# Four small moves in a decoder layer: a residual one tick sooner, the third norm in front of a gate product, epsilon on VectorE, the next input turned in front of the last attend

## The chip, the cores and the metric

The kernel runs on one core of a Trainium2 chip. The metric is the device time of one execution in microseconds; of several executions the median counts.

## The reference

A decoder layer in fp32 over 16 batches of 128 tokens and 256 channels, with three parts, each behind a LayerNorm and added to a residual:

```python
x = x + attn(layernorm(x))             # r, k, v, g from inputs mixed with the token before; 32 heads of 8
x = x + xattn(layernorm(x), ctx)       # causal softmax attention on ctx, 16 heads of 16
x = x + ffn(layernorm(x))              # 8 experts of 176, top 2 of them, and a shared one of 704
# layernorm: (x - mean) / sqrt(var + 1e-5)
# attn, inputs: xx = shift(x) - x;  xk = x + xx * maa_k (xv, xr, xg alike)
# attn, heads: att = (r k) * decay; y = att v; group norm per head; y * silu(g) @ Wo
# ffn: silu(x @ gate) * (x @ up), times the expert's weight, @ down
```

## The kernel before

The 16 batches are worked off in four waves (`g` = 0 to 3) of four batches, 512 tokens. A wave goes through the first attention, the cross attention and the router. The feed-forward part of wave `g - 1` is cut into 34 pieces of 128 hidden rows (`FN` = 34, 17 for each half of 256 tokens) and dealt out between the steps of wave `g`, as *ticks*. That of the last wave runs behind everything, on its own. Each engine has its program written out by hand, in order; `point(g, name)` is the place at which an engine does the ticks that `COUNT` gives to that name. The points are n0 to n5, then x0a, x0b, x0c and so on to x3c for the four batches of the cross attention, then y0 and r0 to r3. Wave 0 has no ticks; there the points do the splitting of the feed-forward weights into high and low parts.

A tick n is a chain over the engines. TensorE does the gate and up products of piece n (L1001 to L1003, 12 products), then the down products of piece n - 2 (L1039 to L1041). ScalarE takes the silu (L772), VectorE multiplies by the up part (L1442, called the gate product here), POOL multiplies by the expert's weight (L612), ScalarE makes the high part (L762), POOL the low part (L601), and that is what the down products wait for. The down products of a half of 17 pieces add up in one PSUM bank. VectorE adds them to the residual when the half is done (L1437), and the first down product of the next half waits for that, since it starts the same bank anew.

The cross attention does, for each batch, scores, maxima, exponentials (ScalarE, L879), the causal selection (POOL, L666) and the product `attend` (TensorE, L1249). On VectorE `attended` takes a reciprocal (L1558) and a multiplication (L1560) that write `yT`. The output projection (TensorE, L1177) waits for `yT` of all four batches. In between, the input of the next wave is made ready: normalised, transposed on TensorE (`turn_norm`, L962, 8 products into banks 2 and 3), then copied by ScalarE (L722) and VectorE (L1384), and `input_differences` subtracts the neighbouring tokens on VectorE (L1386, L1388). The copies wait for `edge_zero`, a memset of the edge column on POOL (L552), which POOL does behind its ticks of x3c.

A LayerNorm takes statistics on VectorE (`bn_stats`, `bn_aggr`), adds epsilon on POOL (L542), raises to the power -0.5 on POOL (L544) and applies mean and factor on VectorE (L1358). The third norm of a wave comes behind the output projection; its result is transposed too (L962), and makes the input of the feed-forward part: `xTf` high by ScalarE (L905), low by VectorE (L1612). Behind the transposes TensorE does the down products of pieces 31 and 32 and the first projection of the next wave (L997), and later the router's product (L1298).

Of the kernel before, what the change touches and what calls it, by code (L numbers as in the profile page):

```python
# [17 lines left out]
def decoder_layer(nc, x, ctx_in, Wr, br, Wk, bk, Wv, bv, Wg, bg, Wo, bo, ln_g, ln_b,  # L18
# [11 lines left out]
    GB = 4  # L30
# [7 lines left out]
    FN = 2 * FB  # L38
    TICKS = FN + 3
    LN_EPS = 1e-5  # L40
# [4 lines left out]
    with es:  # L45
# [341 lines left out]
        POINTS = ["n0", "n1", "n2", "n3", "n4", "n5"] + [f"x{b}{p}" for b in range(GB) for p in "abc"] + ["y0", "r0", "r1", "r2", "r3"]  # L387
        COUNT = dict(n0=1, n1=2, n2=2, n3=2, n4=2, n5=1, y0=1, r0=2, r1=1, r2=1, r3=2)
        for b in range(GB):
# [112 lines left out]
        def _(pool):  # L502
# [35 lines left out]
            def layer_rstd(s, g):  # L538

                i = 0 if s == 0 else 1  # L540
                pool.wait_ge(ln_mean[s], g * 4 + 4)
                pool.tensor_scalar(ve[:, i, :], mv[:, i, :, 1], LN_EPS, None, ALU.add).then_inc(ln_var[s], 1)  # L542
                pool.wait_ge(ln_var[s], g + 1)
                pool.tensor_tensor(rstd[:, i, :], ve[:, i, :], mhalf[:], ALU.pow).then_inc(ln_rstd[s], 1)  # L544
# [391 lines left out]
        def _(pe):  # L936
# [135 lines left out]
            for g in range(NG):  # L1072
# [180 lines left out]
                if g == 0:  # L1253
                    query_scores(0)
                    query_scores(1)
                    for b in (0, 2):
                        turn_maxima(b)
                        key_scores(b)
                        turn_maxima(b + 1)
                        key_scores(b + 1)  # L1260
                        attend(b)
                        attend(b + 1)
                        if b == 0:
                            query_scores(2)
                            query_scores(3)
                else:
                    for b in range(GB):
                        query_scores(b)
                        point(g, f"x{b}a")
                        turn_maxima(b)  # L1270
                        point(g, f"x{b}b")
                        key_scores(b)
                        point(g, f"x{b}c")
                        attend(b)

                if g + 1 < NG:
                    turn_norm(0, g + 1, tokx, 2)
                point(g, "y0")
# [50 lines left out]
        def _(dve):  # L1329
# [10 lines left out]
            def half_means(s, g, q):  # L1340
                i = 0 if s == 0 else 1
                dve.wait_ge(ln_stats[s], g * 4 + 2 * q + 2)
                for b in (2 * q, 2 * q + 1):
                    nc.vector.bn_aggr(mv[:, i, b, :], st[:, i, b, :]).then_inc(ln_mean[s], 1)

            def layer_stats(s, g, src):
# [4 lines left out]
                for b in range(GB):  # L1351
                    nc.vector.bn_aggr(mv[:, i, b, :], st[:, i, b, :]).then_inc(ln_mean[s], 1)

            def layer_apply(s, g, src, dst):
# [77 lines left out]
            def ffn_tick(f, n):  # L1432
                if n - 3 in (FB - 1, FN - 1):
                    half = (n - 3) // FB
                    dve.wait_ge(down_done, f * FN + (half + 1) * FB)
# [18 lines left out]
            for g in range(NG):  # L1454
# [108 lines left out]
                if g == 0:  # L1563
# [10 lines left out]
                    point(g, "x2a")  # L1574
                    attended(2)
                    attended(3)
                else:
                    for b in range(GB):
# [6 lines left out]
                        if b == 2 and g + 1 < NG:  # L1585
                            layer_apply(0, g + 1, tokx, tokx)
                        point(g, f"x{b}c")
                        attended(b)
                point(g, "y0")
                if g + 1 < NG:  # L1590
                    input_differences(g + 1)

# [8 lines left out]
                if g + 1 < NG:  # L1601
                    mixed_input(g + 1, 0)
                if g:
                    ffn_tick(g - 1, ticks_at(g, "r0")[1])
                layer_apply(2, g, X, tok2)
                point(g, "r1")
# [93 lines left out]
```

## Time and profile before

| | |
|---|---|
| median of three runs | 670.97 us (670.49 to 671.01) |
| profiled execution | 671.46 us; span from first to last instruction 669.7 us |
| mean granted TensorE clock | 0.985 |
| TensorE (PE) busy | 621.6 us, 93% |
| VectorE (DVE) busy | 382.8 us, 57% |
| GpSimd (POOL) busy | 342.1 us, 51% |
| ScalarE (ACT) busy | 269.3 us, 40% |

Only TensorE is busy nearly all the time. An engine that is busy for half of the span matters where TensorE waits for it. The granted clock is given as a share of full speed; 0.5 is the lower of its two levels, 1.2 GHz instead of 2.4.

### The profile page before, as it was taken

The page shows a single profiled execution, that of the slowest core. Times are in us where ns is not written, and L with a number is a line of the kernel's source. Part 1 is how long each engine was busy: PE and PEld are TensorE (multiplying, and loading weights), DVE is VectorE, ACT ScalarE, POOL GpSimd, SP SyncE. Part 2 cuts the span into 40 slices and gives each one's busy share as a digit, 9 for nine tenths or more (in the row PEclk, how much of TensorE's full clock was granted, in tenths as well). Part 3 has the DMA queues.
Part 4 walks back from the last instruction along what each step waited for, and adds up shares of the span by engine and source line. Part 5 has one row for each costly group of instructions (what it writes and reads, how often), then busy time and mean ns, then how long its engine had stood idle before and what let it go on. Part 6 is the DMA issues. An engine that isn't in the chain of part 4 may idle for free.

```text
span 669.7 us, 16176 instructions
## 1 busy us (share of the span) xinstructions
PE 621.6 (93%) x6680; PEld 496.7 (74%) x6680; DVE 382.8 (57%) x780; ACT 269.3 (40%) x608; POOL 342.1 (51%) x468
## 2 busy tenths in 40 slices
PE   7987977799999899999999899999999999999996
PEld 6544455445989799755888799854798889899996
DVE  5997778678734453769642544769752444552220
ACT  3857123132335455242325545342324545343332
POOL 7583164214445656514455565615364545518766
PEclk8999978899999999899999999999999999999999
DMA  7921000010121111002031111002011111015220
GB/s 193 357 56 33 1 1 2 1 63 7 39 71 37 42 55 42 5 17 65 27 86 26 38 56 41 21 16 66 18 54 35 37 44 52 21 36 123 70 69 16
DMA packets 41827, 34.13 MB, mean 51 GB/s; under 512 B 9901, under 2 KB 41206, under 8 KB 41754
## 3 DMA queue, kind: packets, MB, share of 16 engines
q1 hardware_dynamic: 39850, 31.27, 16.7%
q10 hardware_dynamic: 1904, 1.84, 0.8%
q8 instruction: 52, 0.85, 0.5%
q14 instruction: 21, 0.17, 0.1%
HBM read 30.92 MB, written 2.17 MB: 49 GB/s over the span
## 4 chain that ended last, share of the span: by engine, by line
PE 47%; DVE 20%; POOL 14%; ACT 8%; issue 8%; DMA 2%; ACTq 0%; POOLq 0%; DVEq 0%
PE bank L997 7%; DVE A L1467 6%; PE bank L1001 4%; DVE nm L1544 3%; POOL A L689 3%; PE bank L1002 3%; PE bank L1003 3%; POOL hT_last L698 3%; PE bank L1177 3%; POOL hb L612 3%; PE bank L1249 3%; PE bank L1039 3%; ACT A L879 2%; PE bank L994 2%; PE bank L1194 2%
## 5 line engine op out<-in xcount | busy, mean ns | idle before, releaser
L1442 DVE TENSOR_TENSOR hb<-hb,bank 128x256 f32<-128x256 f32 (+1 forms) x102 | 42.7, 419 | 144.5 <-ACT hb L772 144.1
L612 POOL TENSOR_TENSOR hb<-hb,cwb 128x256 f32<-128x256 f32 (+1 forms) x102 | 76.4, 749 | 79.1 <-DVE hb L1442 79.0
L601 POOL TENSOR_TENSOR hT<-hb,hT 128x256 fp32r<-128x256 f32 (+1 forms) x102 | 79.3, 778 | 73.2 <-ACT hT L762 73.2
L762 ACT ACTIVATE hT<-hb 128x256 fp32r<-128x256 f32 (+1 forms) x102 | 42.4, 416 | 122.9 <-POOL hb L612 122.3
L1001 PE MATMUL bank<-xTf,wGh 128*128 128x256 f32 x272 | 83.1, 305 | 0.0
L1467 DVE TENSOR_TENSOR A<-bank,decay 128x512 f32<-128x512 f32 x128 | 77.2, 680 | 7.0 <-PE bank L1095 7.0
L1002 PE MATMUL bank<-xTf,wGh 128*128 128x256 f32 x272 | 76.7, 282 | 0.0
L1003 PE MATMUL bank<-xTf,wGl 128*128 128x256 f32 x272 | 76.6, 282 | 0.0
L1002 PE MATMUL bank<-xTf,wUh 128*128 128x256 f32 x256 | 72.2, 282 | 0.0
L1003 PE MATMUL bank<-xTf,wUl 128*128 128x256 f32 x256 | 72.1, 282 | 0.0
L1001 PE MATMUL bank<-xTf,wUh 128*128 128x256 f32 x256 | 72.1, 282 | 0.0
L566 POOL TENSOR_TENSOR A<-A,mcol 128x512 f32<-128x512 f32 x32 | 34.9, 1098 | 72.5 <-PE bank L1095 63.1
L1039 PE MATMUL bank<-wDh,hT 128*128 128x256 f32 (+1 forms) x204 | 59.8, 293 | 5.5 <-DVE res L1437 4.7
L772 ACT ACTIVATE hb<-bank 128x256 f32<-128x256 f32 (+1 forms) x102 | 38.2, 374 | 60.5 <-PE bank L1003 60.1
L1040 PE MATMUL bank<-wDl,hT 128*128 128x256 f32 (+1 forms) x204 | 57.7, 283 | 0.0
L1041 PE MATMUL bank<-wDh,hT 128*128 128x256 f32 (+1 forms) x204 | 57.6, 282 | 0.0
L1001 PEld LDWEIGHTS bank<-xTf,wGh 128*128 128x128 f32 x272 | 51.4, 189 | 8.3 <-issue 5.6
L1002 PEld LDWEIGHTS bank<-xTf,wGh 128*128 128x128 f32 x272 | 51.4, 189 | 0.2
L1003 PEld LDWEIGHTS bank<-xTf,wGl 128*128 128x128 f32 x272 | 51.1, 188 | 0.0
L1001 PEld LDWEIGHTS bank<-xTf,wUh 128*128 128x128 f32 x256 | 48.3, 189 | 0.0
L1002 PEld LDWEIGHTS bank<-xTf,wUh 128*128 128x128 f32 x256 | 48.2, 188 | 0.0
L1003 PEld LDWEIGHTS bank<-xTf,wUl 128*128 128x128 f32 x256 | 48.1, 188 | 0.0
(210 smaller groups left out, 1407.9 us busy)
## 6 DMA issues: line engine op xcount, KB each, us to landing
cwb<-cw_rows SPq DMA_DIRECT2D x54, 128.0 KB, 2.9
A<-cw_rows SPq DMA_DIRECT2D x18, 128.0 KB, 3.4
A<-in_x SPq DMA_DIRECT2D x4, 512.0 KB, 4.5
res<-in_x SPq DMA_DIRECT2D x4, 512.0 KB, 4.1
out_x<-res SPq DMA_DIRECT2D x8, 256.0 KB, 2.5
rawG<-in_L_ffn_w_gate SPq DMA_DIRECT2D x2, 704.0 KB, 6.2
rawU<-in_L_ffn_w_up SPq DMA_DIRECT2D x2, 704.0 KB, 6.6
cwb<-cw_rows SPq DMA_DIRECT2D x12, 112.0 KB, 2.6
```

Source lines behind the costliest of these rows:

```text
L601: pool.tensor_tensor(hT[hr, c % 2, 1, :], hb[hr, c % 2, :], hT[hr, c % 2, 0, :].bitcast(F32), ALU.subtract).then_inc(h_lo, 1)
L612: pool.tensor_tensor(hb[hr, c % 2, :], hb[hr, c % 2, :], cwb[hr, c % CWS, :], ALU.mult).then_inc(h_scaled, 1)
L762: act.activation(hT[hidden(n), c % 2, 0, :], hb[hidden(n), c % 2, :], ACT.Copy).then_inc(h_hi, 1)
L997: last = mm(bank[:, :], wA[:, i, k, m * P:(m + 1) * P], xm[:, c % 4, :], start=k == 0, stop=k == 1)
L1001: mm(out_ap, wh, xh, start=start, stop=False, skip_group_check=skip)
L1002: mm(out_ap, wh, xl, start=False, stop=False, skip_group_check=skip)
L1003: return mm(out_ap, wl, xh, start=False, stop=stop, skip_group_check=skip)
L1039: mm(o, hi[:, t], wDh[hr, j, :], start=(j == 0 and b == 0), stop=False, skip_group_check=True)
L1040: mm(o, hi[:, t], wDl[hr, j, :], start=False, stop=False, skip_group_check=True)
L1041: last = mm(o, lo[:, t], wDh[hr, j, :], start=False, stop=j == FB - 1, skip_group_check=True)
L1442: tt(h, h, up_part(PS[5 + c % 2], n), ALU.mult).then_inc(gu_used, 1)
L1467: tt(att[:, (u % 2) * 4 + i, :].rearrange("p (j t) -> p j t", j=4), PS[SCORE_BANKS[(4 * u + i) % 7]][:, :].rearrange("p (j t) -> p j t", j=4),
```

## The change

The kernel has four edits. The residual of a half is added in tick n - 2 = 16 (or 33), not n - 3, on VectorE, and the count of ticks falls by the one that held the second residual. Epsilon is added by VectorE, right behind the means. The transposes of the next input stand in front of the last attend on TensorE, and the differences in front of the last `attended` on VectorE. `layer_apply(2)` stands in front of the second gate product of r0.

```diff
-    TICKS = FN + 3
+    TICKS = FN + 2
...
-        COUNT = dict(n0=1, n1=2, n2=2, n3=2, n4=2, n5=1, y0=1, r0=2, r1=1, r2=1, r3=2)
+        COUNT = dict(n0=1, n1=2, n2=2, n3=2, n4=2, n5=1, y0=1, r0=2, r1=1, r2=1, r3=1)
...
             def layer_rstd(s, g):
...
-                pool.wait_ge(ln_mean[s], g * 4 + 4)
-                pool.tensor_scalar(ve[:, i, :], mv[:, i, :, 1], LN_EPS, None, ALU.add).then_inc(ln_var[s], 1)
...
                         attend(b)
+                        if b == 2:
+                            turn_norm(0, 1, tokx, 2)
                         attend(b + 1)
...
                         point(g, f"x{b}c")
+                        if b == GB - 1 and g + 1 < NG:
+                            pe.wait_ge(p_exp, g * 16 + 16)
+                            turn_norm(0, g + 1, tokx, 2)
                         attend(b)
 
-                if g + 1 < NG:
-                    turn_norm(0, g + 1, tokx, 2)
                 point(g, "y0")
...
+                if q:
+                    dve.wait_ge(ln_mean[s], g * 4 + GB)
+                    ts(ve[:, i, :], mv[:, i, :, 1], LN_EPS, None, ALU.add).then_inc(ln_var[s], 1)
...
             def ffn_tick(f, n):
-                if n - 3 in (FB - 1, FN - 1):
-                    half = (n - 3) // FB
+                if n - 2 in (FB - 1, FN - 1):
+                    half = (n - 2) // FB
...
                     attended(2)
+                    input_differences(1)
                     attended(3)
...
                         point(g, f"x{b}c")
+                        if b == GB - 1 and g + 1 < NG:
+                            input_differences(g + 1)
                         attended(b)
                 point(g, "y0")
-                if g + 1 < NG:
-                    input_differences(g + 1)
...
                 if g + 1 < NG:
                     mixed_input(g + 1, 0)
+                layer_apply(2, g, X, tok2)
                 if g:
                     ffn_tick(g - 1, ticks_at(g, "r0")[1])
-                layer_apply(2, g, X, tok2)
```

The first place is VectorE at point x1c of wave 1, where the first half ends. The row that writes `res` is the residual, those that write `hb` are gate products, and `mv` are the means of the next input. Before:

```order
L1352 BN_AGGR mv<-st 128x2 x3
L1442 TENSOR_TENSOR hb<-hb,bank 128x256 [waits silu_done]
L1437 TENSOR_TENSOR res<-bank,res 128x512 [waits down_done]
L1442 TENSOR_TENSOR hb<-hb,bank 128x256 [waits silu_done]
L1558 RECIPROCAL S<-bank 128x256 [waits yT_ready,o_part]
```

And in the changed kernel:

```order
L1356 BN_AGGR mv<-st 128x2 x3
L1358 TENSOR_SCALAR ve<-mv 128x4 [waits ln_mean0]
L1443 TENSOR_TENSOR res<-bank,res 128x512 [waits down_done]
L1448 TENSOR_TENSOR hb<-hb,bank 128x256 [waits silu_done] x2
L1564 RECIPROCAL S<-bank 128x256 [waits yT_ready,o_part]
```

The residual has moved in front of the first of the two gate products, and the addition of epsilon has come in behind the means.

The second place is VectorE at the end of the cross attention of wave 1, from the gate products of x3 to the first addition behind the output projection. The copy, and the two subtractions behind it, are `input_differences`; reciprocal and multiplication are `attended(3)`. Before:

```order
L1442 TENSOR_TENSOR hb<-hb,bank 128x256 [waits silu_done] x5
L1558 RECIPROCAL S<-bank 128x256 [waits yT_ready,o_part]
L1560 TENSOR_TENSOR A<-bank,S 128x2x128 [waits rec_ready]
L1442 TENSOR_TENSOR hb<-hb,bank 128x256 [waits silu_done]
L1384 COPY A<-bank 128x4x128 [waits edge_zero,xn_turned0]
L1386 TENSOR_TENSOR A<-A 128x512 [waits xnT_act]
L1388 TENSOR_TENSOR A<-A 128x512 [waits xnT_dve]
L1595 TENSOR_TENSOR res<-bank,res 128x512 [waits wout_ready]
```

And in the changed kernel:

```order
L1448 TENSOR_TENSOR hb<-hb,bank 128x256 [waits silu_done] x5
L1390 COPY A<-bank 128x4x128 [waits edge_zero,xn_turned0]
L1392 TENSOR_TENSOR A<-A 128x512 [waits xnT_act]
L1394 TENSOR_TENSOR A<-A 128x512 [waits xnT_dve]
L1564 RECIPROCAL S<-bank 128x256 [waits yT_ready,o_part]
L1566 TENSOR_TENSOR A<-bank,S 128x2x128 [waits rec_ready]
L1448 TENSOR_TENSOR hb<-hb,bank 128x256 [waits silu_done]
L1602 TENSOR_TENSOR res<-bank,res 128x512 [waits wout_ready]
```

The three instructions have moved past `attended(3)` and the gate product of y0.

The third place is VectorE behind the output projection of wave 1, from the last means to the gate product of r1 (its 64 rows are the short last piece). The rows that read `rstd` are the third norm. Before:

```order
L1344 BN_AGGR mv<-st 128x2
L1442 TENSOR_TENSOR hb<-hb,bank 128x256 [waits silu_done]
L1396 SCALAR_TENSOR_TENSOR A<-A,cols 128x512 [waits xx_ready]
L1442 TENSOR_TENSOR hb<-hb,bank 128x256 [waits silu_done]
L1358 TENSOR_SCALAR A<-res,mv,rstd 128x256 [waits ln_rstd2]
L1358 TENSOR_SCALAR A<-res,mv,rstd 128x256 x3
L1442 TENSOR_TENSOR hb<-hb,bank 64x256 [waits silu_done]
```

And in the changed kernel:

```order
L1345 BN_AGGR mv<-st 128x2
L1348 TENSOR_SCALAR ve<-mv 128x4 [waits ln_mean2]
L1448 TENSOR_TENSOR hb<-hb,bank 128x256 [waits silu_done]
L1402 SCALAR_TENSOR_TENSOR A<-A,cols 128x512 [waits xx_ready]
L1364 TENSOR_SCALAR A<-res,mv,rstd 128x256 [waits ln_rstd2]
L1364 TENSOR_SCALAR A<-res,mv,rstd 128x256 x3
L1448 TENSOR_TENSOR hb<-hb,bank 128x256 [waits silu_done]
L1448 TENSOR_TENSOR hb<-hb,bank 64x256 [waits silu_done]
```

The norm and one gate product have changed places, and epsilon has come in behind the means.

## Rows read from the trace of the kernel before

**Rows 1.** The page, part 1: busy us (share of the span) xinstructions.

```profile
PE 621.6 (93%) x6680; PEld 496.7 (74%) x6680; DVE 382.8 (57%) x780; ACT 269.3 (40%) x608; POOL 342.1 (51%) x468
```

**Rows 2.** Waits, whole span: engine, line, releaser, total us, times, longest.

```profile
PE bank L1039 <- DVE res L1437: 4.7, 3, 1.6
```

**Rows 3.** Timeline, residual, wave 1: start, us, engine, line, idle before.

```profile
224.92 0.28 PE L1041 MATMUL bank<-wDh,hT 64*128 64x256 f32 x1
...
227.30 0.42 DVE L1442 TENSOR_TENSOR hb<-hb,bank 128x256 f32<-128x256 f32 x1 [3.31 <-ACT hb L772]
...
228.37 0.38 PE L1039 MATMUL bank<-wDh,hT 128*128 128x256 f32 x1 [1.54 <-DVE res L1437]
```

**Rows 4.** Timeline, wave 0, between two select groups on POOL.

```profile
90.47 1.19 POOL L542 TENSOR_SCALAR ve<-mv 128x4 f32<-128x4 f32 x1
...
93.32 2.39 POOL L666 TENSOR_SCALAR_AFFINE_SELECT pexB<-pexB 128x512 f32<-128x512 f32 x4
...
95.77 0.64 PE L1249 MATMUL bank<-pexB,A 128*32 128x128 f32 x16 [1.58 <-POOL pexB L666]
```

**Rows 5.** Timeline, wave 2, end of the attention.

```profile
419.21 1.09 PE L962 MATMUL bank<-ident,A 128*128 128x128 f32 x8
...
420.51 0.12 POOL L552 MEMSET A<- 128x8 f32 x1
...
421.46 0.42 DVE L1560 TENSOR_TENSOR A<-bank,S 128x256 f32<-128x256 f32 x1
...
422.28 3.61 PE L1177 MATMUL bank<-wX,A 128*128 128x256 f32 x16
...
422.53 0.68 DVE L1384 COPY A<-bank 128x512 f32<-128x512 f32 x1
...
424.49 0.68 DVE L1595 TENSOR_TENSOR res<-bank,res 128x512 f32<-128x512 f32 x1
```

**Rows 6.** Timeline, wave 0, end of the attention.

```profile
113.88 0.11 POOL L552 MEMSET A<- 128x8 f32 x1
...
113.95 1.76 DVE L1558 RECIPROCAL S<-bank 128x256 f32<-128x256 f32 x1
...
116.32 3.69 PE L1177 MATMUL bank<-wX,A 128*128 128x256 f32 x16 [1.83 <-DVE A L1560]
```

**Rows 7.** Timeline, wave 2, third norm.

```profile
428.12 0.74 DVE L1396 SCALAR_TENSOR_TENSOR A<-A,cols 128x512 f32<-128x512 f32 x1
...
428.28 1.50 POOL L544 TENSOR_TENSOR rstd<-ve,mhalf 128x4 f32<-128x4 f32 x1
...
431.58 1.79 DVE L1358 TENSOR_SCALAR A<-res,mv,rstd 128x256 f32<-128x256 f32 x4
...
432.05 0.44 PE L962 MATMUL bank<-ident,A 128*128 128x128 f32 x2 [1.16 <-DVE A L1358]
...
433.10 0.85 POOL L601 TENSOR_TENSOR hT<-hb,hT 128x256 fp32r<-128x256 f32 x1 [0.53 <-ACT hT L762]
...
435.12 3.60 PE L997 MATMUL bank<-A,wA 128*128 128x512 f32 x8
```

**Rows 8.** Timeline, wave 0, third norm on POOL.

```profile
121.90 0.63 POOL L542 TENSOR_SCALAR ve<-mv 128x4 f32<-128x4 f32 x1 [7.91 <-DVE mv L1344]
...
122.61 1.05 POOL L544 TENSOR_TENSOR rstd<-ve,mhalf 128x4 f32<-128x4 f32 x1
```

**Rows 9.** Timeline, wave 3, behind the third norm.

```profile
586.76 1.09 ACT L905 ACTIVATE xTf<-bank 128x512 fp32r<-128x512 f32 x2 [0.61 <-PE bank L962]
...
588.83 1.06 PE L1298 MATMUL bank<-xTf,wR 128*10 128x128 f32 x32 [0.67 <-DVE xTf L1612]
```

**Rows 10.** Timeline of wave 1 on PE; then a window: us, busy, clock, DMA.

```profile
267.08 3.62 PE L1177 MATMUL bank<-wX,A 128*128 128x256 f32 x16
...
281.01 4.06 PE L997 MATMUL bank<-A,wA 128*128 128x512 f32 x8
...
279.00:282.00 3.00, 3.00 (x13) 0.51 0.03 5
```

More of the change, by code:

```diff
@@ L1352, in layer_stats @@
                     nc.vector.bn_aggr(mv[:, i, b, :], st[:, i, b, :]).then_inc(ln_mean[s], 1)
+                dve.wait_ge(ln_mean[s], g * 4 + GB)
+                ts(ve[:, i, :], mv[:, i, :, 1], LN_EPS, None, ALU.add).then_inc(ln_var[s], 1)
             def layer_apply(s, g, src, dst):
```

## The prediction

> **What bounds the kernel now.** I read the page first: TensorE is busy for 621.6 of 669.7 us [rows 1]. So only two things can move the end: time in which TensorE stands still, and time in which its clock is low. The list of waits shows where it stands still. The largest entry there that this change touches is L1039, the down product that opens a half, waiting for the residual on VectorE: 4.7 us in three waits [rows 2]. I then read the timeline at the four edited places, each time asking what TensorE waits for last. Times below are of the profiled execution (671.46 us, span 669.7); the median of the three timed runs is 670.97. I make the sum as a difference and take it off the median. I call the four groups of batches waves 0 to 3.
>
> **Part 1, the residual one tick sooner.** In wave 1 the last product of down(16) starts at 224.92 and ends at 225.20. VectorE stands idle for 3.31 us before the gate product at 227.30, does the residual only behind it, and down(17) starts at 228.37 after a wait of 1.54 us [rows 3]. An addition of this shape takes 0.68 us [rows 5]. In front of that gate product it can run from 225.3 to 226.0, so the gate product still starts at 227.30, and down(17) finds its bank free. The whole wait goes. The two later waves have it too, in all 4.7 us [rows 2]. Everything up to the end of the attention follows TensorE, so I let it pass through in full: **-4.7**. Only the first half moves; the second residual was already the last thing of its wave.
>
> **Part 2, epsilon on VectorE.** Of the twelve norms most keep POOL's small addition hidden under other work. At one place in wave 0 it isn't: at 90.47 POOL does it for 1.19 us, between two groups of selects, and TensorE waits 1.58 us for the second group, at 95.77 [rows 4]. On VectorE the addition ends before POOL is free. That gives back 1.19 us and the gap behind it, less what the wait of 1.58 leaves: **-1.2**. VectorE pays 0.2 us of idle time.
>
> **Part 3, the next input turned in front of the last attend.** On TensorE nothing is added: eight transposes, 0.85 us, change places with the attend product. On VectorE the three steps of the differences now stand in front of the reciprocal and the multiplication that make yT, and yT is what the output projection L1177 waits for. In wave 2 the differences cannot start before POOL's memset of the edge, 420.51 to 420.63 [rows 5]. From the copy at 422.53 to the next instruction at 424.49 they take 1.96 us [rows 5]. So they run from 420.7 to 422.7; the reciprocal takes 1.76 us [rows 6] and the multiplication 0.42, and yT is ready at 424.9 instead of 421.88. L1177 could start at 425.05; before it started at 422.28 with no wait [rows 5]. That is 2.77 us in wave 2, and the same in wave 1. In wave 0 the memset ends at 113.99 and the reciprocal had started at 113.95; it now starts at 115.9, so L1177 moves from 116.32 [rows 6] to 118.25: 1.9 us. Wave 3 has no next input. Together **+7.4**. What hid the differences before was the projection itself, and that cover is gone. They gave VectorE little to catch up: it was late for the projection's halves by 0.2 us at most.
>
> **Part 4, the third norm ahead of a gate product.** I count from the start of L1177. In waves 0 and 3 the means are ready 5.5 us behind it: in wave 0 POOL's addition starts at 121.90, 5.58 us behind 116.32 [rows 6, 8]. With the addition on VectorE (an estimated 0.2 us, small VectorE steps being about that), the power starts at 5.8. It takes 1.50 us in wave 2 [rows 7], so it ends at 7.3. The norm's four instructions took 1.79 us from 431.58, which is 9.30 behind L1177 [rows 7]; now they start at 7.3 and end at 9.1. TensorE gets to the transposes at 8.6 (432.05 less the 1.16 it waited) and is done with them at 9.5, not 11.3. But the displaced gate product now starts at 9.1, against 8.97 before, and its path through POOL and ScalarE ends in L601, which in wave 2 ended at 433.95, so 11.67 [rows 7]. Its down product, the second behind the transposes, must wait for that: TensorE is there at 10.2 and waits 1.5 us. The next projection, L997, starts at 12.4 behind L1177, against 12.84 (435.12 less 422.28) [rows 5, 7]. So wave 2 gets 0.4 us and not the 1.9 of the norm: the stall moves one product on.
>
> Wave 1 was different. There L997 started 13.93 us behind L1177 and took 4.06 instead of 3.60 us, because the granted clock fell to 0.51 in that window (the 1.2 GHz level) after TensorE had stood still in front of the transposes [rows 7, 10]. With that idle gone I count 1.53 + 0.46: 2.0 us. In wave 3 ScalarE waited only 0.61 us for the turned norm and then the gate chain binds, so 0.6 us [rows 9]. In wave 0 the addition took 0.63 us [rows 8] and now 0.2, but the power, 1.05 us there [rows 8], will run beside the mixed input's instruction L1396, as it did in wave 2: there L1396 ran from 428.12 and the power took 1.50 us [rows 7]: the two cancel, 0.1. Together **-3.1**.
>
> The Trainium skill, GPSIMD Engine Reference, section 8 (Key points), says that GpSimd shares its SBUF interfaces with VectorE and suffers from VectorE instructions with two SBUF inputs. By that rule alone wave 0's norm gives 0.1 us; by the row of the addition alone it would give 0.5 us, and the sum would be lower by 0.4 us. The trace agrees, with 1.05 us against 1.50 us for one and the same power.
>
> **Part 5, the clock.** The change makes TensorE stand still where it did not: 3.7 us in wave 0 in front of L1177 (1.83 before [rows 6], plus 1.9), and 2.7 us in waves 1 and 2. In this trace 1.54 us of idle in front of L1039 cost no clock, 1.16 us and 0.3 more in front of the transposes did in wave 1 and did not in wave 2 [rows 3, 7, 10]. Such a drop is worth 1.5 us: (13.93 - 12.84) + (4.06 - 3.60) [rows 5, 7, 10]. Bounds: none, 0; one in each of the three places, 4.6, and a fourth behind the new wait of part 4, 6.2. I take one, in wave 0, the longest idle: **+1.5**.
>
> **Sum.** -4.7 - 1.2 + 7.4 - 3.1 + 1.5 = -0.1 us. On the median: 670.9 us. So four edits, of which one costs nearly what the others bring.
>
> **The rivals.**
> *Faster: the clock doesn't fall.* Then the sum is -1.6, and 669.4 us. For it: waves 1 and 2 show that the same idle needn't bring a drop. It could go further if POOL's memset came sooner than part 3 has it: 0.5 us of that is worth 1.5 us over three waves, down to 667.9. Against it: the memset stands behind POOL's product in program order, and nothing moved there. Chance 0.30.
> *Slower: the turned input decides.* The one mechanism is the idle that part 3 makes in front of L1177, priced with the low clock in waves 1 and 2 as well: +3.0 on the forecast, 673.9 us. It decides from the second drop on, where the time passes 672.3. For it: 2.7 us is more than any idle of waves 1 to 3 now. Against: part of such a drop is spent beside the POOL chain of part 4, which TensorE waits for anyway. Chance 0.27.
> *The residual doesn't get its 4.7.* If down(16) ended later than VectorE's gate product could start, the gate chain would wait for the residual, and only part of each 1.54 would go. At half, the sum is +2.2, 673.2 us. The rows leave 1.3 us of room (226.0 against 227.30) [rows 3], so I give it 0.03.
>
> **How the numbers follow.** My forecast, a sum near nothing, has 0.40: its own range is 669.6 to 672.3. A measurement of this kernel tells about 0.2%, 1.34 us, from no change, so the forecast is "same". The faster rival has 0.30, slower and the residual together 0.30. The range for 8 in 10 runs from 667.9, the end of the faster case, to 673.9, the middle of the slower one.
>
> **What would show it.** Part 1: L1039 no longer in the waits for the residual. Part 2: no small addition on POOL, and the second group of selects of wave 0 starting 1.2 us sooner. Part 3: L1177 waiting for yT for about 2.7 us in waves 1 and 2 and 3.7 in wave 0, with the edge memset as what the copy waits for. Part 4: next to no wait in front of the norm's transposes, and a wait of about 1.5 us at L1039 for POOL's L601 behind them. Part 5: windows at about half clock behind L1177. The prediction is wrong if L1177 does not wait (670.9 less 7.4 is 663.5), or if the drops are three or more.

## The result and the profile after

| | before | changed |
|---|---|---|
| median of 18 runs each | 671.09 us | 675.78 us |
| lowest and highest | 670.39, 675.62 | 674.81, 680.71 |
| span of the profiled execution | 669.7 us | 673.9 us |
| mean granted clock | 0.985 | 0.985 |

The ratio is 1.007, with a 95% interval of 1.0054 to 1.0087: the change made the kernel slower by 4.7 us, where the forecast was -0.1 us. The prediction was wrong, and the time lies above 673.9 us, the end of its range.

The list of waits of the changed kernel, TensorE's entries (total us, times, longest), which answers to [rows 2]:

```profile
PE bank L1175 <- DVE A L1566: 11.6, 4, 4.8
...
PE bank L1037 <- POOL hT L599: 4.3, 6, 1.2
PE bank L960 <- DVE A L1364: 4.0, 1, 4.0
```

L1175 is the output projection now, L1566 the multiplication that makes yT. The wait for the residual is gone, and so is the one in front of the norm's transposes (L960), wave 0's excepted. In their place stand 11.6 us at the output projection. That the entry for the residual vanished and that the kernel became slower are both true, so the sum of waits has to be read place by place. The timeline of wave 1 at the end of the attention answers to [rows 5]:

```profile
266.03 0.11 POOL L550 MEMSET A<- 128x8 f32 x1
266.24 0.69 DVE L1390 COPY A<-bank 128x512 f32<-128x512 f32 x1 [0.96 <-POOL A L550]
266.87 0.69 DVE L1392 TENSOR_TENSOR A<-A 128x512 f32<-128x512 f32 x1
267.22 0.93 POOL L599 TENSOR_TENSOR hT<-hb,hT 128x256 fp32r<-128x256 f32 x1 [1.07 <-ACT hT L760]
267.48 1.22 DVE L1394 TENSOR_TENSOR A<-A 128x512 f32<-128x512 f32 x1
268.62 1.75 DVE L1564 RECIPROCAL S<-bank 128x256 f32<-128x256 f32 x1
270.40 0.42 DVE L1566 TENSOR_TENSOR A<-bank,S 128x256 f32<-128x256 f32 x1
...
270.97 5.38 PE L1175 MATMUL bank<-wX,A 128*128 128x256 f32 x16 [3.11 <-DVE A L1566]
```

Two things are to be seen. VectorE's five steps run one behind the other from POOL's memset to yT, and TensorE waits 3.11 us for them. And then the 16 products of the projection take 5.38 us, where they took 3.62 [rows 10]. The windows of the changed kernel around the projection, in waves 0, 1 and 2, show why (the column before the last two is the granted clock, the last two are DMA):

```profile
117.00:120.00 3.00, 2.98 (x8) 2.49 (x9) 0.00 (x0) 0.00 (x0) 0.00 (x0) 0.59 0.00 0
...
270.00:273.00 3.00, 2.03 (x5) 1.69 (x6) 1.12 (x3) 0.42 (x1) 1.24 (x2) 0.69 0.00 0
273.00:276.00 3.00, 3.00 (x13) 2.44 (x12) 1.34 (x3) 0.00 (x0) 0.21 (x1) 0.74 0.07 22
...
429.00:432.00 3.00, 3.00 (x9) 2.37 (x8) 1.69 (x5) 0.00 (x0) 0.49 (x1) 0.58 0.12 22
```

The clock is at its lower level (1.2 GHz) for part of each of them. Waves 0 and 2 have the same row for the projection:

```profile
117.02 5.38 PE L1175 MATMUL bank<-wX,A 128*128 128x256 f32 x16 [4.80 <-DVE A L1566]
...
427.25 5.38 PE L1175 MATMUL bank<-wX,A 128*128 128x256 f32 x16 [3.10 <-DVE A L1566]
```

So there are three drops at this place, each worth 5.38 - 3.69 = 1.7 us in the projection itself, where the forecast had one. The rest of the comparison is a walk along TensorE's timeline. Shown is by how much each mark stands later than in the kernel before.

| mark on TensorE | later than before, us |
|---|---|
| projection of wave 0, 117.02 | +0.70 |
| router's product of wave 0, 132.90 | +2.37 |
| projection of wave 1, 270.97 | +3.89 |
| router's product of wave 1, 289.37 | +3.47 |
| projection of wave 2, 427.25 | +4.97 |
| router's product of wave 2, 445.65 | +6.09 |
| projection of wave 3, 580.13 | +4.43 |
| router's product of wave 3, 592.97 | +4.14 |

### The profile page after: what moved, and what is told of

It reads as the page before. It is cut to its first block, busy times and chain, and to the rows that moved or that the text cites. A ratio compares the mean times of both kernels' runs of the same rounds, so it can differ in the third digit from the quotient of the medians.

```text
span 673.9 us, 16178 instructions
## 1 busy us (share of the span) xinstructions
PE 620.5 (92%) x6680; PEld 496.6 (74%) x6680; DVE 386.4 (57%) x792; ACT 268.9 (40%) x608; POOL 336.7 (50%) x456
## 3 DMA queue, kind: packets, MB, share of 16 engines
q1 hardware_dynamic: 39850, 31.27, 17.3%
## 4 chain that ended last, share of the span: by engine, by line
PE 32%; DVE 24%; POOL 17%; issue 12%; ACT 11%; DMA 2%; ACTq 0%; POOLq 0%; DVEq 0%
PE bank L995 7%; DVE A L1473 6%; DVE nm L1550 5%; POOL hb L610 5%; POOL A L687 3%; DVE S L1564 3%; POOL hT_last L696 3%; ACT A L877 3%; POOL hT L599 3%; PE bank L1175 3%; ACT L770 2%; ACT L791 2%; PE bank L992 2%; PE bank L1192 2%; DVE hb L1448 2%
## 5 line engine op out<-in xcount | busy, mean ns | idle before, releaser
L599 POOL TENSOR_TENSOR hT<-hb,hT 128x256 fp32r<-128x256 f32 (+1 forms) x102 | 78.9, 773 | 72.8 <-ACT hT L760 72.8
```

The source lines that it names most:

```text
L599: pool.tensor_tensor(hT[hr, c % 2, 1, :], hb[hr, c % 2, :], hT[hr, c % 2, 0, :].bitcast(F32), ALU.subtract).then_inc(h_lo, 1)
```

## The experiments

Each kernel below was timed in five rounds beside the kernel before, on the same chip as that; the kernels come in three groups, each with its own chip and its own times of the kernel before. One measure is used in most of them: the **stretch** from the first product of the output projection to the router's product (L1298 before, L1299 after) on TensorE. It holds the projection, the third norm's transposes, the down products and half of the next wave's first projection, and whether the clock fell in it can be read from its length alone.

| kernel | median us | ratio to before, 95% interval | stretch, wave 0 / 1 / 2, us |
|---|---|---|---|
| before | 671.09 | | 14.21 / 18.82 / 17.28 |
| changed | 675.78 | 1.007 [1.0054, 1.0087] | 15.88 / 18.40 / 18.40 |
| all but part 3 | 662.79 | 0.9873 [0.9853, 0.9893] | 14.85 / 16.82 / 16.83 |
| part 3 alone | 684.68 | 1.0199 [1.0175, 1.0223] | 15.65 / 18.40 / 18.42 |
| changed, waits at the projection filled | 671.06 | 1.0 [0.9977, 1.0024] | 14.75 / 16.71 / 16.73 |
| changed, memset earlier | 669.69 | 0.9976 [0.9954, 0.9998] | 15.88 / 16.72 / 16.75 |
| part 1 alone | 665.31 | 0.9906 [0.9881, 0.9932] | 14.10 / 17.28 / 18.84 |
| part 4 alone | 671.06 | 0.9994 [0.997, 1.0018] | 14.20 / 17.44 / 17.42 |
| part 2 alone | 667.61 | 0.9933 [0.9907, 0.9959] | no usable trace |
| part 2 alone, again | 667.70 | 0.9932 [0.9912, 0.9952] | 14.90 / 16.67 / 16.69 |
| parts 1 and 2 | 664.38 | 0.9875 [0.9845, 0.9906] | 14.19 / 16.66 / 16.68 |
| changed, but differences late | 663.29 | 0.9886 [0.985, 0.9921] | 16.60 / 16.73 / 16.72 |
| all but part 3, norm's wait filled | 660.72 | 0.9839 [0.9812, 0.9865] | 12.50 / 16.82 / 16.83 |
| the same, a second wait filled | 661.06 | 0.984 [0.9811, 0.9869] | 12.50 / 16.83 / 16.85 |

The kernel before measured 671.97 us beside the third to the sixth row, 671.39 beside the next three and the one with the norm's wait filled, and 672.81 beside the others, so the ratios are what to compare. There is one trace of each kernel, and of one execution; a stretch tells of that execution only.

### Is it part 3, and what of it?

All but part 3 (from the changed kernel):

```diff
-                            turn_norm(0, g + 1, tokx, 2)
                         attend(b)
+                if g + 1 < NG:
+                    turn_norm(0, g + 1, tokx, 2)
...
-                            input_differences(g + 1)
                         attended(b)
                 point(g, "y0")
+                if g + 1 < NG:
+                    input_differences(g + 1)
```

> The changed kernel with its fourth edit undone: transposes and differences of the next input are back behind the last attend. Theory: the turned input costs 1.96 us of wait in wave 0 and 3.1 us in each of waves 1 and 2, and a low clock behind each of the three waits, 1.6 to 1.8 us apiece; everything else in the change is a gain of some 9 us (residual 4.7, epsilon 1.3, third norm 3). Then this kernel takes about 662 us, ratio 0.987. Rival: the other edits brought little, and what is lost comes from the third norm (its displaced gate product) or the residual. Then this kernel stays within 0.3% of the kernel before.

And part 3 alone, the same lines the other way round in the kernel before:

> The kernel before with the fourth edit alone. Theory: waits of 8.2 us and three drops of the clock, 5.1 us, less the drop of wave 1 at the third norm that the kernel before has already (1.5 us): +11 to +13 us, ratio 1.017 to 1.020. Rival (the loss is in the waits alone and the clock costs nothing that isn't waited for anyway): +7 to +8 us, ratio 1.011. Rival (the other edits cost as well): under +5 us, ratio below 1.008.

Measured: 662.79 us, a ratio of 0.9873, and 684.68 us, 1.0199. So parts 1, 2 and 4 together bring 9.2 us by the medians and 8.5 by the ratio (forecast 9.0), and part 3 costs some 13 us (0.0199 and 0.0197 of the time before) whether it is put on the kernel before or on the one with the other parts. The forecast gave part 3 and the clock together 7.4 + 1.5 = 8.9 us. The trace of part 3 alone, the fastest of its six executions, is only 10.4 us longer than that of the kernel before (680.1 and 669.7): in it the third norm of wave 1 has no drop of the clock, which the kernel before has there.

The traces with and without part 3 on top of the others (673.9 and 660.7 us) show where the 13.2 us between them lie. Up to the projection, which holds the wait for yT, it adds 2.25 us in wave 0, 3.31 in wave 1 and 3.33 in wave 2, 8.9 us in all, where the forecast had 1.9 + 2.77 + 2.77 = 7.4. In the stretches behind the projection's start, which hold the lower clock, it adds 1.03, 1.58 and 1.57, 4.2 us in all, where the forecast had 1.5.

The next kernel is the changed one with the idle time in front of the projection filled: 20 products of 512 columns into an unused bank in wave 0, 12 in waves 1 and 2. The output is the same.

```diff
                 point(g, "y0")
+                if g + 1 < NG:
+                    idle_product(12 if g else 20, 0 if g else 7)
                 pe.wait_ge(yT_ready, g * 4 + 4)
```

> The changed kernel with idle products on TensorE in front of the output projection's wait: 20 in wave 0 and 12 in waves 1 and 2, bf16 128x512, into a bank that the projection (or nobody) writes next. They fit inside the waits of 4.8 and 3.1 us (0.22 us each by wave 0's idle products), so the waits stay and only the idleness goes; the output is unchanged. Theory: the granted clock stays at 1.00 behind all three and the projection takes 3.6 us again instead of 5.4: 1.6 to 1.8 us three times, so 670.5 to 671.5 us, ratio 1.000. Rival (the slow projection is hidden by the POOL chain behind the norm, or has another cause): 675.8 us, ratio 1.007, with or without a low clock.

Measured: 671.06 us, 1.0 [0.9977, 1.0024], against 1.007 for the changed kernel. Its trace has in wave 1, with a window behind the projection's start:

```profile
272.32 2.76 PE L969 MATMUL bank<-identb 128*128 128x512 bf16 x12
...
275.58 3.69 PE L1175 MATMUL bank<-wX,A 128*128 128x256 f32 x16 [0.50 <-DVE A L1568]
...
276.00:279.00 3.00, 3.00 (x17) 2.64 (x15) 1.38 (x3) 0.42 (x1) 1.29 (x2) 1.00 0.07 22
```

TensorE still can't start the projection before yT is there, but does it in 3.69 us, at a granted clock of 1.00. Filling the wait doesn't shorten it; it gives back 1.7 us in each stretch of waves 1 and 2 and 1.13 us in wave 0's, and 4.7 us by the medians. In wave 0 the 20 products were too many: yT is ready at 121.95 in this trace and the projection starts at 122.81, behind the last of them. So 4.7 us is rather too little for the clock. The lower clock is one part of what part 3 costs, and the wait itself the other. (The profiled execution of this kernel took 677.01 us, above its median; it was late already, by 3 us at wave 0's first projection, and I read only the stretches in it.)

The next kernel shortens the wait instead. POOL does the edge memset in front of its ticks of x3c and not behind them, so that VectorE's copy starts as soon as the transposes are there.

```diff
                     if b == 0 and g == 0:
                         layer_rstd(0, g + 1)
+                    if b == GB - 1 and g + 1 < NG:
+                        zero_edge(g + 1)
                     point(g, f"x{b}c")
...
-                if g + 1 < NG:
-                    zero_edge(g + 1)
                 point(g, "y0")
```

> The changed kernel with POOL's memset of the edge column moved in front of its ticks of x3c (in wave 0 in front of the weight splitting there). Theory: VectorE's copy waited 0.96 us for it in waves 1 and 2 and 1.79 us in wave 0, so yT comes that much sooner: 3.5 to 3.7 us less than the changed kernel, 672 us, ratio 1.0015, the clock still falling each time. If the shorter idle of wave 1 and 2 (2.2 us) no longer brings the clock down, another 1.7 us each goes. Rival (the copy would wait for something else, or yT doesn't set the projection): no change, 675.8 us.

Measured: 669.69 us, 0.9976 [0.9954, 0.9998], some 6 us less than the changed kernel. In wave 1:

```profile
268.79 3.69 PE L1175 MATMUL bank<-wX,A 128*128 128x256 f32 x16 [1.66 <-DVE A L1566]
...
270.00:273.00 3.00, 3.00 (x18) 2.72 (x17) 2.14 (x6) 0.23 (x1) 0.73 (x1) 1.00 0.17 22
```

An idle time of 1.66 us is left, the clock stays up, and wave 2 is the same with 1.67 us. In wave 0, 3.46 us are left and the projection takes 5.38 us, as in the changed kernel. The expectation had this only as its second case, and with 2.2 us of idle left, not 1.66.

The last kernel of this group keeps TensorE's half of part 3 and puts VectorE's half back: transposes in front of the last attend, differences behind the last `attended`.

```diff
                     attended(2)
-                    input_differences(1)
...
-                            input_differences(g + 1)
                         attended(b)
                 point(g, "y0")
+                if g + 1 < NG:
+                    input_differences(g + 1)
```

> The changed kernel with half of part 3 undone: TensorE's transposes stay in front of the last attend product, but VectorE does the differences behind the last multiplication, as before. Theory (all that part 3 costs comes from what stands in front of the reciprocal on VectorE): as without part 3, 662.8 us, a ratio of 0.9873. Rival (the transposes in front of the attend product cost their own 0.85 us in each of three waves, since the attend product ends so much later and yT with it): 665.3 us, 0.991.

Measured: 663.29 us, 0.9886 [0.985, 0.9921]; the intervals overlap with those without part 3, and the rival's 0.991 is inside too. The timeline is sharper: from the router's product of one wave to the projection of the next it takes 135.14 and 134.93 us in waves 1 and 2, against 134.76 and 134.55 without part 3. That is 0.38 us each, less than half of the 0.85 us of the transposes. Nearly all that part 3 costs in these waves is VectorE's order. Wave 0 is less clean: in this trace its projection starts behind 2.43 us of idle and takes 5.38 us, where without part 3 it had 1.41 and 3.69. (The profiled execution, 668.01 us, was above the median; four of the six took 663.0 to 663.4 us, so this trace needn't stand for them.)

### What the other parts are worth one by one

Part 1 alone (`n - 3` to `n - 2`, `TICKS` and `r3` less by one, in the kernel before):

> The kernel before with part 1 alone: the residual in tick n - 2. Theory (the wait of 4.7 us for the residual goes and passes through in full): 4.7 us less than before, a ratio of 0.993, and no wait of the down products for the residual in the list of waits. Rival (only the wave in which it was seen, 1.6 us, passes through, the others being given back at the third norm): 0.9975.

Measured: 0.9906, 6.3 us by the ratio, against 4.7 expected. By the marks of its trace waves 1, 2 and 3 gain 1.75, 1.80 and 1.63 us between the router's product of one and the projection of the next, 5.2 us; the other 0.7 us of its span lie in wave 0, which the edit doesn't touch. What I had not expected is in the stretches: wave 1's fell from 18.82 to 17.28 us, and wave 2's rose from 17.28 to 18.84. The rows of this kernel, waves 1 and 2, and a window of wave 2:

```profile
274.34 0.44 PE L962 MATMUL bank<-ident,A 128*128 128x128 f32 x2 [1.15 <-DVE A L1358]
...
277.42 3.60 PE L997 MATMUL bank<-A,wA 128*128 128x512 f32 x8
...
426.20 0.44 PE L962 MATMUL bank<-ident,A 128*128 128x128 f32 x2 [1.16 <-DVE A L1358]
...
429.00:432.00 3.00, 3.00 (x12) 2.26 (x11) 2.75 (x4) 0.73 (x2) 1.24 (x2) 0.65 0.03 8
```

The same wait of 1.15 us (and 0.29 more) stands in both waves of both kernels. It brings the clock down in wave 1 of the kernel before and in wave 2 of this one, 1.5 us each time. Whether a short wait brings a drop isn't decided by its length alone. With one trace of each kernel it isn't shown either that part 1 moved the drop: two executions of one kernel might differ in the same way.

Part 4 alone (`layer_apply(2)` in front of the second gate product of r0, in the kernel before):

> The kernel before with part 4 alone: the third norm in front of the gate product, epsilon still on POOL. Theory (the stall moves one product on, wave 1 keeps its clock): 2 to 3 us less than before, a ratio of 0.996, with TensorE waiting in waves 1 and 2 about 1 us at the down products for POOL's low part and not at the transposes. Rival (the wait behind the norm is as long as the one that it replaces): no change, 1.000.

Measured: 0.9994 [0.997, 1.0018], the rival's number. The wait moves as foreseen, to 1.25 us at the down product in wave 1:

```profile
280.70 0.40 PE L1039 MATMUL bank<-wDh,hT 128*128 128x256 f32 x1 [1.25 <-POOL hT L601]
```

Wave 1's stretch falls by 1.38 us, which is its clock drop, but wave 2's, which had none, grows by 0.14 us. Its executions ranged from 668.97 to 674.2 us, and wave 0 of the profiled one was 0.9 us longer up to the projection, so a gain of 1.4 us would be hard to see in its median. By the trace, then, the reordering itself brings nothing in these waves; the clock drop that went with it was the only gain.

Part 2 alone (epsilon behind the means on VectorE, in the kernel before):

> The kernel before with part 2 alone: epsilon on VectorE. Theory: 1.2 us in wave 0 and some tenths in front of the third norm's power, 1.2 to 2 us less in all, a ratio of 0.9975. Rival (the power, now beside VectorE's instructions, stretches by what the addition saved): 1.000. If the three terms are separate, the changes of this kernel and of the two with part 1 and part 4 alone add up to the 9.2 us of the kernel with all three.

Measured: 667.61 us, 0.9933, 3.8 us by the medians and twice what I expected at most. The execution that was traced took 2052.3 us, so the kernel was measured once more for its trace:

> The kernel with part 2 alone once more, for its trace: it gave 0.9933 where theory had 0.9975. Theory: beside the 1.2 us of wave 0, the norm's result comes so much sooner in wave 1 that the clock no longer falls behind the wait in front of the transposes, which frees another 1.5 us there; then wave 1's stretch from the output projection to the router's product is 17.3 us and not 18.82. Rival: the gain is all in wave 0's cross attention, where the slow stretches of the clock lie elsewhere; then the stretch in wave 1 is still 18.8 us.

Measured: 667.70 us, 0.9932. Wave 1's stretch is 16.67 us, below even the 17.3 expected. The rows of wave 1:

```profile
272.31 1.01 POOL L542 TENSOR_TENSOR rstd<-ve,mhalf 128x4 f32<-128x4 f32 x1 [3.01 <-DVE ve L1345]
...
275.12 1.79 DVE L1361 TENSOR_SCALAR A<-res,mv,rstd 128x256 f32<-128x256 f32 x4
...
275.58 0.44 PE L960 MATMUL bank<-ident,A 128*128 128x128 f32 x2 [0.55 <-DVE A L1361]
```

The power takes 1.01 us here and not 1.50. It starts 0.16 us ahead of L1399, the mixed input's instruction (272.47), where in the kernel before it started 0.16 us behind it (428.28 and 428.12 in wave 2 [rows 7]). All traces agree with this as the reason. Where the mixed input's instruction started first, the power took 1.45 to 1.50 us (15 times, wave 0 of the kernels with epsilon on VectorE among them); where the power started first, be it by 0.02 us as in the kernel with part 3 alone, it took 1.01 to 1.05 us (20 times). In wave 0 of the changed kernel:

```profile
124.31 0.74 DVE L1402 SCALAR_TENSOR_TENSOR A<-A,cols 128x512 f32<-128x512 f32 x1
124.48 1.45 POOL L542 TENSOR_TENSOR rstd<-ve,mhalf 128x4 f32<-128x4 f32 x1 [11.75 <-DVE ve L1348]
```

So epsilon on VectorE brings more than its own length in waves 1 and 2: it lets the power start in front of that instruction. The norm starts 8.70 us behind the projection and not 9.30 [rows 5, 7], TensorE waits 0.55 us for it and not 1.15, and the clock stays up. That is 0.6 us in waves 1 and 2 each and the drop's 1.5 us in wave 1, besides 1.4 us in front of wave 0's projection. Wave 0's own stretch gives 0.7 us back in this trace, but not in that of parts 1 and 2 (14.19), which has the same program there.

Parts 1 and 2 without 3 and 4:

> Parts 1 and 2 without 3 and 4. Theory (part 4 is worth about 0.45 us in each of waves 1 and 2 once the clock drop of wave 1 is gone, since the stall moves on to the down product): 1 us more than parts 1, 2 and 4 together, a ratio of 0.9888. Rival (part 4 is worth the 3.1 us of the prediction): 0.992.

Measured: 664.38 us, 0.9875 [0.9845, 0.9906], the same as with part 4 (0.9873). The stretches are 16.66 and 16.68 us without it, 16.82 and 16.83 with it. Once epsilon is off POOL, the third norm in front of the gate product costs 0.15 us in waves 1 and 2 each, and gives 0.1 us back in wave 3. Both expectations had it bring something.

### The clock at the other waits

All but part 3, with 14 idle products in wave 0's wait of 4.03 us in front of the third norm's transposes:

```diff
+                if g == 0:
+                    idle_product(14, 7)
                 turn_norm(2, g, tok2, 0)
```

> Parts 1, 2 and 4 without the turned input, and 14 idle products on TensorE in wave 0's wait of 4.03 us in front of the third norm's transposes, the last long idle with a clock drop behind it. The output is unchanged. Theory (such a drop costs 1.6 us wherever it falls): 1.6 us less than without the idle products, 661.2 us, a ratio of 0.985 to before. Rival (what stands behind, the copies and the router, binds there and not the clock): 662.8 us, 0.9873.

Measured: 660.72 us, 0.9839 [0.9812, 0.9865], the best of the kernels here: 2.3 us less than without, by the ratios. Wave 0's stretch fell from 14.85 to 12.50 us. In its trace:

```profile
120.78 3.18 PE L969 MATMUL bank<-identb 128*128 128x512 bf16 x14
124.98 1.41 PE L960 MATMUL bank<-ident,A 128*128 128x128 f32 x8 [1.01 <-DVE A L1363]
126.22 3.60 PE L995 MATMUL bank<-A,wA 128*128 128x512 f32 x8
```

L995 takes 3.60 us, where it took 5.44 without the idle products, and the transposes 1.41 and not 1.97. So this drop cost 2.4 us, and not the 1.6 that the expectation gave to each.

And the same with 10 more, in front of the second attend product of wave 0, where TensorE waits for POOL's second group of selects:

```diff
                         attend(b)
+                        if b == 0:
+                            idle_product(10, 1)
                         attend(b + 1)
```

> Parts 1, 2 and 4 with idle products in two waits of wave 0: 14 in front of the third norm's transposes as in the kernel with 0.9839, and 10 more in the wait of 2.7 to 3.7 us for POOL's second group of selects, in front of the second attend product. The output is unchanged. Theory (that wait lets the clock fall in some executions and not in others): 0 to 2 us less than with the one wait filled, 659.5 us, 0.982, and the attend products of wave 0 take 0.62 and not 1.10 us a group. Rival (VectorE and POOL bind there, not the clock): 660.7 us, 0.984.

Measured: 661.06 us, 0.984 [0.9811, 0.9869]: no gain that can be told, the rival's number. Its reason isn't shown, for the kernel doesn't test it well. In its trace:

```profile
90.65 3.27 POOL L664 TENSOR_SCALAR_AFFINE_SELECT pexB<-pexB 128x512 f32<-128x512 f32 x4
...
92.55 2.39 PE L969 MATMUL bank<-identb 128*128 128x512 bf16 x10
...
94.86 0.64 PE L1247 MATMUL bank<-pexB,A 128*32 128x128 f32 x16
```

The selects end at 93.92, but the attend product starts at 94.86, when the idle products are through: ten were too many, and cost 0.9 us. Nor need it be their doing that the groups behind them take 0.62 to 0.64 us. In the traces of wave 0 the slow groups come either in front of this wait or behind it. In nine of them, this one included, groups of the first attend product took up to 0.99 to 1.08 us, and all of the second 0.62 to 0.65. In the other four the first took 0.62 to 0.64, the wait was 3.26 to 3.70 us, and the second went up to 1.08 or 1.10. The slow groups behind the wait are not free: with them VectorE's reciprocal starts 3.41 us behind the second attend product (98.41 and 95.00 in the trace of 0.9839), and 2.03 us here. Whether fewer idle products would keep the slow groups away, and gain, is untested.

## Why the prediction was wrong, by its own steps

**Part 5, the clock, is the step that failed.** It took one drop, in wave 0, and named three as a bound. There were three at the output projection. Filling the waits took these away, and the ratio went from 1.007 to 1.000. By the traces with and without part 3, the clock cost 4.2 us net of what was waited for anyway, against the forecast's 1.5, and is 2.7 of the 4.3 us that the two traces of before and changed lie off the forecast. Another 1.5 us is part 3's own wait, mis-sized. The reason that it gave against drops in waves 1 and 2 was that 1.54 and 1.16 us of idle had mostly cost no clock [rows 3, 7, 10]. That was an argument from waits half as long. The trace of before has a longer one, which the forecast left out: 4.16 us in wave 0, in front of the third norm's transposes, with the first projection slow behind it:

```profile
124.17 1.70 PE L962 MATMUL bank<-ident,A 128*128 128x128 f32 x8 [4.16 <-DVE A L1358]
125.66 4.93 PE L997 MATMUL bank<-A,wA 128*128 128x512 f32 x8
```

Nothing in that trace lies between 1.83 and 4.16 us at these two places, so the price of 2.7 us of idle had to be guessed. In the traces of all the kernels the unfilled waits of 2.43, 2.96, 3.10, 3.11, 3.46, 4.80 and 4.82 us at the output projection had a drop behind them, and those of 1.94, 1.92, 1.83, 1.67, 1.66 and 1.41 us had none. At the norm's transposes 4.03 us had one, and 1.15 us two in four. That is no rule of length: at wave 0's second attend product 2.78 us in the changed kernel had none, where the clock had been low shortly before. The rival "slower" had the mechanism right; the forecast gave it a chance of 0.27, at 673.9 us, still 1.9 us too low, mostly since it too went by 7.4 us for the waits.

**Part 3 was right in kind and too small by 0.34 us a wave** in waves 1 and 2: 3.11 and 3.10 us of idle where it worked out 2.77. The projection itself moved by 3.31 and 3.33 us, 0.55 more than forecast, and by 2.25 us in wave 0, 0.35 more. The second subtraction, L1394, takes 1.22 us and not 0.68, with POOL's L599 beside it, itself 0.93 us and not 0.73. The projection of wave 0 starts with 4.80 us of idle and not 3.7: TensorE was there sooner, since the transposes no longer stand behind the attend product.

The Trainium skill, GPSIMD Engine Reference, section 8 (Key points), says that GpSimd and VectorE share SBUF interfaces and that VectorE instructions with two SBUF inputs bring contention. The trace agrees, and shows that it goes both ways: 1.22 and not 0.68 us for VectorE's subtraction, 0.93 and not 0.73 us for POOL's low part. Which of the two pays goes with which starts first. Here L599 starts 0.26 us ahead of the subtraction. In the kernel before the subtraction L1388 starts 0.06 us ahead of L601, takes 0.68 us, and L601 takes 1.21.

**Part 1 held.** The wait is gone, and the three waves give 5.2 us in the kernel with part 1 alone, against 4.7. In the changed kernel VectorE has the residual at 227.62, in front of the gate product, as foreseen:

```profile
227.62 0.69 DVE L1443 TENSOR_TENSOR res<-bank,res 128x512 f32<-128x512 f32 x1 [0.76 <-PE bank L1039]
229.69 0.42 DVE L1448 TENSOR_TENSOR hb<-hb,bank 128x256 f32<-128x256 f32 x1 [1.38 <-ACT hb L770]
```

**Parts 2 and 4 were right in their sum and wrong in their shares.** The forecast had -1.2 and -3.1; alone they measured -3.8 and -0.3 by the medians, and the three parts together 9.2 us against 9.0. That this sum came out so close is luck: it adds a part worth three times its price to one worth a tenth. What I had put down to the new place of the norm, the 2.0 us of wave 1, is got by epsilon alone. I had looked at wave 0 only for part 2, and had the small addition hidden elsewhere; it stood in front of the power in every wave. Part 4 also took 1.50 us for the power in waves 1 and 2, where it takes 1.01 with epsilon on VectorE; in wave 0, where it foresaw 1.50, it takes 1.45. The three parts alone bring 6.3 + 4.5 + 0.4 = 11.2 us by their ratios and 8.5 together by theirs. 1.5 us of that is wave 1's clock drop, which is gone in the traces of part 2 and of part 4 and is there once; the rest is inside the intervals, of some 1.7 us either way for each. At wave 0's second attend product TensorE starts 1.25 us sooner (94.52 and 95.77), but it was 0.32 us ahead already at the transposes in front of the cross attention (72.87 and 73.19), so POOL gave back 0.93 us of the forecast's 1.2. Its power took 2.30 us there and not 1.60:

```profile
88.91 2.30 POOL L542 TENSOR_TENSOR rstd<-ve,mhalf 128x4 f32<-128x4 f32 x1
...
91.19 3.28 POOL L664 TENSOR_SCALAR_AFFINE_SELECT pexB<-pexB 128x512 f32<-128x512 f32 x4
...
94.52 0.64 PE L1247 MATMUL bank<-pexB,A 128*32 128x128 f32 x16 [2.78 <-POOL pexB L664]
```

The wait that part 4 foresaw at the second down product is there, 1.2 us for L599 (forecast 1.5), six times 4.3 us in all with the smaller ones.

What stays open: which of the short waits (1.15 us) brings a drop. It stood in the other wave in the trace with part 1, where the norm's transposes come 2.5 us sooner in wave 1 and 5.9 us sooner in wave 2. And wave 0's cross attention takes 1 to 3 us longer in the traces in which the slow attend groups come behind the wait for the selects, also between kernels that have the same program up to there. I haven't settled what decides that, and single parts are known no better than that.

## What to carry to other kernels

Work that is moved in front of a step that the busiest engine waits for is paid twice where that engine is TensorE: once as the wait, and once as the lower clock behind it, here 3.1 us of idle and 1.6 us of stretch in each of waves 1 and 2. Before moving it, find the waits in the trace that are as long as the new one or longer, and look at the clock behind those, here the 4.16 us of wave 0; don't price it by the shorter ones. When several edits touch one stall, only the kernels with one edit each tell whose gain it is: here epsilon on VectorE had it, and the norm's new place had nothing.

## What the runs showed of the hardware

- A drop of the granted clock cost 1.5 to 1.7 us in the projection behind each of its waits of 2.43 to 4.82 us, whatever the length: its 16 products took 5.21 to 5.38 us, against 3.61 to 3.69 behind waits of up to 1.94 us. Idle products in the wait took the drop away. At the third norm's transposes in wave 0, behind 4.03 us, a drop cost 2.4 us.
- The same wait of 1.15 us and 0.29 us had a drop behind it in one wave and not in another, and the two stood the other way round in the trace with part 1 added.
- A power of 128 x 4 elements on POOL took 1.00 to 1.05 us in most places, also where VectorE's mixed input started 0.02 to 0.16 us behind it; 1.45 to 1.50 us where that instruction (0.74 us) had started first; 1.60 us in wave 0's cross attention with VectorE's splitting beside its first part, and 2.30 to 2.38 us with it beside the whole.
- A subtraction of 128 x 512 on VectorE and the low part of 128 x 256 on POOL, begun 0.06 us apart with VectorE first, took 0.68 and 1.21 us; begun 0.26 us apart with POOL first, 1.22 and 0.93 us.
- VectorE's addition of epsilon took 0.17 to 0.64 us, against 0.23 to 1.19 us on POOL.
